# A graph attention layer: the first two weight tiles side by side, another order of ScalarE's and GpSimd's work in a pair step, evacuation by halves

## What is computed

```python
# x: 384 x 1024, 16 heads of 64, 6144 edges
q = x @ wq.T + bq ; k = x @ wk.T + bk ; v = x @ wv.T + bv
q2 = (q @ wiq.T + biq).reshape(N, H, D).transpose(1, 0, 2)
k2 = (k @ wik.T + bik).reshape(N, H, D).transpose(1, 0, 2)
v2 = (v @ wiv.T + biv).reshape(N, H, D).transpose(1, 0, 2)
mask = full((N, N), -inf); mask[src, dst] = softplus(edge_weights)[edge_type - 1]   # the diagonal is always set
scores = einsum('hnd,hmd->hnm', q2, k2) / 8 + mask
out = einsum('hnm,hmd->hnd', softmax(scores), v2).transpose(1, 0, 2).reshape(N, 1024)
return layernorm(x + out @ wo.T + bo)
```

## Time and profile before

| | us |
|---|---|
| median of 3 (306.43 to 307.05) | 306.74 |
| the profiled execution | 306.56 |
| its span, first to last instruction | 304.8 |
| TensorE busy / DVE / ACT / GpSimd | 291.7 / 204.4 / 175.1 / 147.8 |
| granted TensorE clock, share of full | 0.999 |

### The profile page before, as it was taken

The page is one execution under the profiler, slowest core; times in us unless marked ns, Lnnn a source line. Parts: engine busy times, 40 slices in busy tenths (PEclk is TensorE's granted clock), DMA queues, the critical chain, the costliest instruction groups (busy, mean ns, idle before and its releaser), DMA issues. The chain is left out here.

```text
span 304.8 us, 5251 instructions
## 1 busy us (share of the span) xinstructions
PE 291.7 (96%) x1640; PEld 272.4 (89%) x1640; DVE 204.4 (67%) x493; ACT 175.1 (57%) x329; POOL 147.8 (49%) x126
## 2 busy tenths in 40 slices
PE   6899999999999999999999999999999997899992
PEld 6789999999999998888989999999999996678882
DVE  4789856676666674305277888888797888763084
ACT  4843443334443342221488898989898989644432
POOL 4100655655546546478653545454544545944600
PEclk9999999999999999999999999999999999999999
DMA  6886745354652438745021222221222221420013
GB/s 191 311 328 246 264 142 190 97 195 139 207 207 85 148 113 329 292 149 197 10 71 61 78 70 70 69 69 69 69 69 69 69 69 71 139 69 0 2 69 138
DMA packets 14030, 39.83 MB, mean 131 GB/s; under 512 B 3168, under 2 KB 4800, under 8 KB 13888
## 3 DMA queue, kind: packets, MB, share of 16 engines
q1 hardware_dynamic: 11984, 38.91, 36.9%
q0 software_dynamic: 1680, 0.62, 1.0%
q10 hardware_dynamic: 352, 0.13, 0.2%
HBM read 37.44 MB, written 2.21 MB: 130 GB/s over the span
## 5 line engine op out<-in xcount | busy, mean ns | idle before, releaser
L328 POOL DMA_INDIRECT mask_cells<-cell_value,cell x48 | 57.0, 1187 | 60.4 <-DMA mask_cells<-cell_value,cell 31.8
L296 POOL TENSOR_TENSOR w_lo<-w_raw,w_hi 128x1024 fp32r<-128x1024 f32 (+2 forms) x22 | 51.1, 2326 | 63.8 <-DVE probs L748 32.4
L853 PE MATMUL bank<-x_hi,w_hi 128*128 128x384 f32 x192 | 64.5, 336 | 2.9 <-POOL w_lo L296 1.6
L384 ACT ACTIVATE w_hi<-w_raw 128x1024 fp32r<-128x1024 f32 x51 | 52.9, 1054 | 20.4 <-PE bank L862 19.4
L855 PE MATMUL bank<-x_hi,w_lo 128*128 128x384 f32 x192 | 64.2, 334 | 0.0
L854 PE MATMUL bank<-x_lo,w_hi 128*128 128x384 f32 x192 | 64.2, 334 | 0.0
L419 ACT ACTIVATE h_hi<-bank,bcol 128x384 f32 (+1 forms) x24 | 14.0, 582 | 59.7 <-PE bank L855 59.7
L587 DVE TENSOR_TENSOR w_lo<-w_raw,w_hi 128x1024 fp32r<-128x1024 f32 (+2 forms) x32 | 38.3, 1201 | 13.6 <-ACT w_hi L384 11.3
L853 PE MATMUL bank<-h_hi,w_hi 128*128 128x384 f32 x128 | 46.4, 362 | 0.0
L855 PE MATMUL bank<-h_hi,w_lo 128*128 128x384 f32 x128 | 43.0, 336 | 0.0
L854 PE MATMUL bank<-h_lo,w_hi 128*128 128x384 f32 x128 | 42.9, 335 | 0.0
(11 more groups left out here) (103 smaller groups left out, 528.3 us busy)
## 6 DMA issues: line engine op xcount, KB each, us to landing
w_raw<-weights SPq DMA_DIRECT2D x56, 512.0 KB
probs<-key_rows SPq DMA_DIRECT2D x6, 512.0 KB
v<-x_t SPq DMA_DIRECT2D x8, 192.0 KB, 5.7
res<-x_rows SPq DMA_DIRECT2D x1, 1536.0 KB, 6.8
out<-res SPq DMA_DIRECT2D x6, 256.0 KB, 2.0
mask_cells<-cell_value,cell POOLq DMA_INDIRECT x48
mask_cells<-mask SPq DMA_DIRECT2D x1, 576.0 KB, 6.0
mask<-mask_cells POOLq DMA_DIRECT2D x1, 576.0 KB, 4.4
```

The source lines that it names most:

```text
L296: nc.gpsimd.tensor_tensor(lo, w_raw[:, s, cols], hi.bitcast(F32), ALU.subtract)\
L328: nc.gpsimd.indirect_dma_start(out=mask_cells, out_offset=bass.IndirectOffsetOnAxis(ap=cell[:, c:c + 1], axis=0), in_=cell_value[:, c:c + ...
L384: nc.scalar.activation(w_part(t, s, slice(0, F))[0], w_raw[:, s, :], ACT.Copy).then_inc(w_hi_done, 1)
L853: pe.matmul(out_ps, w_hi[:, s, cols], moving_hi, start=(k == 0), stop=False)
```

## The change

- Start: tiles 0 and 1 get accumulators of their own (`first_acc`, banks 4 and 5), and TensorE does both for each block of x. They are loaded and split in halves of 512 columns. ACT issues block 0, the first half of tile 1 and block 3; SP the rest, and the edge arrays, the edge weights and the bias columns behind x. Tile 2 is ahead of the edge columns, tile 3 behind the bias columns, and tiles 4 and 5 ahead of the edge keys. DVE does all low parts; all eight counts of the first group come behind the value table and tile 5's low part.
- Pair step: ACT takes five exponentials, splits the odd weight tile (before, this was the step's last work), and takes the sixth. ACT counts each half of q and k that it evacuates (`half_hi`), and DVE waits for one half at a time. GpSimd subtracts the odd weight tile ahead of `att_low`.
- Around the last pair: ACT splits both weight tiles ahead of the exponentials, GpSimd subtracts both ahead of `v_low` and then waits for all six normalised tiles; DVE masks all six score tiles ahead of the normalisations; TensorE projects with tile `WO_TILE + 1` (left half) and does the last value product of pair 6 ahead of the scores, and the first transposes come behind three projections more.

```diff
         acc = bank[6:8]
+        first_acc = bank[4:6]
...
+            def half_tile(t, h):
+                sp.dma_start(w_raw[:, t, HALVES[h]], weights[t, :, HALVES[h]])\
+                  .then_inc((first_half_loaded, raw_loaded)[h][t], 16)
+            def x_block(k):
                 sp.dma_start(x_raw(k), x_t[:, k, :]).then_inc(x_loaded[k], 16)
-            first_tile(1)
+            half_tile(0, 0)
+            x_block(1)
+            x_block(2)
+            half_tile(0, 1)
+            half_tile(1, 1)
+            for k in range(4, KT):
+                x_block(k)
+            sp.dma_start(er[:, :, :], edge_rows).then_inc(edges_loaded, 16)
+            first_tile(2)
+            sp.dma_start(ec[:, :, :], edge_cols).then_inc(edges_loaded, 16)
+            sp.dma_start(ew[:, :], edge_weights.to_broadcast([P, ETYPES])).then_inc(small_loaded, 16)
             sp.dma_start(bcol[:, :], bias_cols).then_inc(small_loaded, 16)
+            first_tile(3)
+            for s in range(FIRST_TILES):
+                load_tile(RING + s, s)
             sp.wait_ge(edge_prep, 1)
             sp.dma_start(key_rows.rearrange("g (c e) -> (g c) e", e=P), er_key[:, :]).then_inc(scratch_stored, 16)
-            first_tile(2)
             sp.wait_ge(scratch_stored, 16)
             load_rows(0, 0)
-            first_tile(3)
-            for s in range(RING):
+            for s in range(FIRST_TILES, RING):
                 load_tile(RING + s, s)
+            sp.wait_ge(rows_loaded, 16)
             load_rows(1, 1)
...
+                low_part(t + LEAD + 1, s0 + 1)
                 if not (isinstance(j, int) and j < 2):
                     att_low(j - 2)
-                low_part(t + LEAD + 1, s0 + 1)
...
             low_part(WO_TILE + 2, 2)
+            low_part(WO_TILE + 3, 3)
             v_low(PAIRS - 1, 1)
-            low_part(WO_TILE + 3, 3)
+            pool.wait_ge(probs_ready, 2 * NT * PAIRS)
...
-            act.dma_start(er[:, :, :], edge_rows).then_inc(edges_loaded, 16)
-            act.dma_start(ec[:, :, :], edge_cols).then_inc(edges_loaded, 16)
-            act.dma_start(ew[:, :], edge_weights.to_broadcast([P, ETYPES])).then_inc(small_loaded, 16)
+            act.dma_start(x_raw(0), x_t[:, 0, :]).then_inc(x_loaded[0], 16)
+            act.dma_start(w_raw[:, 1, HALVES[0]], weights[1, :, HALVES[0]]).then_inc(first_half_loaded[1], 16)
+            act.dma_start(x_raw(3), x_t[:, 3, :]).then_inc(x_loaded[3], 16)
...
+            def first_high(t, h):
+                act.wait_ge((first_half_loaded, raw_loaded)[h][t], 16)
+                nc.scalar.activation(w_hi[:, t, HALVES[h]], w_raw[:, t, HALVES[h]], ACT.Copy)\
+                    .then_inc((first_half_hi, w_hi_done)[h], 1)
+            def x_high(k):
                 act.wait_ge(x_loaded[k], 16)
                 nc.scalar.activation(x_hi[:, k, :], x_raw(k), ACT.Copy).then_inc(x_hi_done, 1)
-            act.wait_ge(raw_loaded[1], 16)
-            for half, done in zip(HALVES, (first_half_hi, w_hi_done)):
-                nc.scalar.activation(w_hi[:, 1, half], w_raw[:, 1, half], ACT.Copy).then_inc(done, 1)
+            first_high(0, 0)
+            x_high(0)
+            first_high(1, 0)
+            for k in range(1, 4):
+                x_high(k)
+            first_high(0, 1)
+            first_high(1, 1)
+            for k in range(4, KT):
+                x_high(k)
+            high_part(2, 2, 1)
...
-                    ins = nc.scalar.activation((q_high, k_parts)[which][here, 2 * slot + h, :],
-                                               acc[which][here, 0:N], ACT.Identity, bias=bcol[here, ds(u, 1)])
-                ins.then_inc(acc_hi, 1)
+                    nc.scalar.activation((q_high, k_parts)[which][here, 2 * slot + h, :], acc[which][here, 0:N],
+                                         ACT.Identity, bias=bcol[here, ds(u, 1)]).then_inc(half_hi, 1)
...
-                    if isinstance(j, int) and j < 2:
-                        exps(a)
-                    else:
+                    if not (isinstance(j, int) and j < 2):
                         att_half_out(a - 1, 1)
-                        exps(a)
-                if attend:
+                    exps(a, range(0, 5))
+                    split(t + LEAD + 1, s0 + 1, raws)
+                    exps(a, range(5, 6))
...
                 evacuate(t + 1, L1_TILES + 1 + 2 * j, par, 1)
                 if attend:
                     att_half_out(a, 0)
-                split(t + LEAD + 1, s0 + 1, raws)
+                else:
+                    split(t + LEAD + 1, s0 + 1, raws)
...
             split(WO_TILE + 2, 2, (WO_TILE + 2) // RING + 1)
+            split(WO_TILE + 3, 3, (WO_TILE + 3) // RING + 1)
             v_high(a, 1)
             att_half_out(a - 1, 1)
-            exps(a, range(0, 3))
-            split(WO_TILE + 3, 3, (WO_TILE + 3) // RING + 1)
-            exps(a, range(3, 6))
+            exps(a)
...
+            first_low(0, 0)
+            x_low(0)
+            first_low(1, 0)
+            for k in range(1, 4):
+                x_low(k)
+            first_low(0, 1)
+            first_low(1, 1)
+            for k in range(4, KT):
+                x_low(k)
...
+            for t in range(FIRST_TILES):
+                low_part(t + LEAD, t + LEAD)
+                evacuate(t, first_acc[t])
+            low_part(FIRST_TILES + LEAD, 0)
+            evacuate(FIRST_TILES, acc[0])
+            value_table()
+            low_part(FIRST_TILES + 1 + LEAD, 1)
+            evacuate(FIRST_TILES + 1, acc[1])
+            dve.wait_ge(rows_loaded, 16)
+            count_later(0, ds(0, 1), range(GC))
+            choose_cells(0)
...
-                dve.wait_ge(acc_hi, u + 1)
                 for h in range(2):
+                    dve.wait_ge(half_hi, 2 * (u - L1_TILES) + (h + 1))
...
+                last = u is None
+                for i in range(6 if last else 5):
                     mask_scores(a, i)
                 normalise(a, (0, 2))
                 normalise(a, (4,))
-                mask_scores(a, 5)
+                if not last:
+                    mask_scores(a, 5)
...
+            for k in range(KT):
+                pe.wait_ge(x_lo_done, k + 1)
+                for t in range(FIRST_TILES):
+                    if k == 0:
+                        pe.wait_ge(first_half_lo, t + 1)
+                    if k == KT // 2:
+                        tile_ready(t)
+                    ins = by_outputs(first_acc[t][:, 0:N], t, k, x_hi[:, k, :], x_lo[:, k, :])
+                    if k == KT - 1:
+                        ins.then_inc(tile_done, 1)
...
             project(0, 0, left)
             for g in range(KT - VALUES_FROM, 2 * NT - 1):
                 values(a - 1, 0, g)
+            project(0, 1, left)
+            values(a - 1, 0, 2 * NT - 1)
             pe.wait_ge(acc_free, L1_TILES + 2 + 2 * PAIRS)
             scores(a, 1, 0)
             project(0, 0, right)
-            values(a - 1, 0, 2 * NT - 1)
             scores(a, 1, 1)
-            project(0, 1)
+            project(0, 1, right)
             scores(a, 1, 2)
             project(0, 2)
             pe.wait_ge(masked, 2 * NT * PAIRS - 1)
             project(1, 0, left)
             project(1, 1, left)
-            transposes(a, 0)
             pe.wait_ge(masked, 2 * NT * PAIRS)
             project(1, 0, right)
             project(1, 1, right)
             project(1, 2)
+            transposes(a, 0)
+            project(0, 3)
             transposes(a, 1)
-            project(0, 3)
             for g in range(4):
                 values(a, 1, g)
                 transposes(a, g + 2)
```

More of the change, by code:

```diff
@@ L49 @@
 LEAD = 2
-FIRST_COLS = 448
-SHARED_TILES = 2
+FIRST_TILES = 2
 WARM_UP = 16
@@ L182, in gnn_layer @@
         q_doubled = sem("q_doubled")
+        first_half_loaded = [sem(f"first_half_loaded{t}") for t in range(FIRST_TILES)]
         first_half_hi, first_half_lo = sem("first_half_hi"), sem("first_half_lo")
         tile_done = sem("tile_done")
-        acc_hi = sem("acc_hi")
+        acc_hi, half_hi = sem("acc_hi"), sem("half_hi")
         acc_free = sem("acc_free")
@@ L293, in low_part @@
                 pool.wait_ge(w_hi_done, t + 1)
-                cols = pool_cols(t) if isinstance(t, int) and t < SHARED_TILES else slice(0, F)
+                cols = slice(0, F)
                 hi, lo = w_part(t, s, cols)
@@ L411, in group @@
                     t = RING * g + s
-                    late = first and s < LEAD
-                    if not late:
+                    if not (first and s == 0):
                         high_part(t + LEAD, (s + LEAD) % RING, g + 1 + (s + LEAD) // RING)
                     act.wait_ge(tile_done, t + 1)
-                    nc.scalar.activation(h_hi[:, ds(t, 1), :].rearrange("p a n -> p (a n)"), acc[s % 2][:, 0:N],
+                    ps = first_acc[s] if first and s < FIRST_TILES else acc[s % 2]
+                    nc.scalar.activation(h_hi[:, ds(t, 1), :].rearrange("p a n -> p (a n)"), ps[:, 0:N],
```

(48 more changed lines are left out.)

49 lines of the change are left out of this document (19 added, 30 removed).

## The result

| | before | after |
|---|---|---|
| median, us (lowest to highest) | 306.89 (306.43 to 307.82, 4 runs) | 299.64 (299.56 to 299.71, 4 runs) |
| ratio, 95% interval | | 0.976 (0.9736 to 0.9783) |
| profiled execution, its span | 306.56, 304.8 | 299.66, 297.9 |
| mean granted clock of TensorE | 0.999 | 0.997 |

The forecast was 299.9. To see where the 7 us are, I cut the timeline of TensorE at four starts that both traces have (L numbers move, the operations don't): tile 6, the transposes of the first pair, those of the last step of the loop, and the last matmul.

What follows compares the result with a forecast made beforehand. TensorE, busy 96% of the span, was taken as the bound, with gains only where it stands still: start 2.4, loop 1.4, last pair 3.0, sum 6.8, from 306.74 to 299.9 us; range 298.6 to 302.6.

Steps and rivals of the forecast that it cites:

- the loop's 1.4: Pair steps: half evacuations let DVE finish k earlier, removing TensorE's 0.24 wait at the scores in six steps, 1.4 us.
- The start: Up to tile 6: DVE's gapless list after ACT's softplus constants sets tile 6 at 32.75 against 35.18, gain 2.4 us.
- The feared queues: Start, SP's queue: small constants landing at 16 would leave 0.3 gain; edge keys' store and read-back expected without stall.
- (a): Start: constants or rows of keys land late and DVE's backlog leaves a gain of 0.3 to 1; 301.7 us, chance 0.13.
- (d): Start: it is not held by DVE's list; 299.1 us, chance 0.07.
- The first pair: First pair: 0.5 won at the scores is given back at the transposes, where ACT's table load and exponentials set time; 0.
- (b): Pair loop: the 0.24 at L927 is a restart cost, not a wait; 1.4 less gain, 301.3 us, chance 0.10.
- the moved split: Pair step: ACT's 1.05 split fits into its idle 1.16 before the sixth exponential; priced at 0.
- (e): Pair steps: the split delays the sixth exponential by 1.05 each step, costing 7.35; 308.7 us, chance 0.04.
- The odd weight tile on GpSimd: Pair step: subtraction moved ahead of att_low gives the weight tile 4 us more cover, att_low 1.8 later; priced at 0.
- The last pair: Last pair: waits at scores (1.88) and transposes (1.75) go, less 0.3 left at the scores and 0.3 later; gain 3.0 us.
- (c): Last pair: GpSimd's gate delays weight tiles and the last projections by 1.5; 301.4 us, chance 0.06.

Runs made afterwards that it cites:

- e10: Kernel before plus the new start and the half evacuations; split, GpSimd's odd weight tile and last pair at their old places: 304.80 us, ratio 0.9924.
- e8: Kernel after, with DVE's evacuation ahead of the first count in every tile of the loop over groups: 299.32 us, ratio 0.9749.
- e1: Kernel before plus the new start alone; pair steps and last pair as before: 304.95 us, ratio 0.9928.
- e7: Kernel after, with a one-column exponential on ACT before the first pair step, so Exp's table loads early: 298.81 us, ratio 0.9735.
- e3: Kernel after, but DVE waits for both halves of q and k before it evacuates the first: 301.61 us, ratio 0.9818.
- e6: Kernel after, with ACT's split of the odd weight tile one exponential earlier, before the fifth: 305.15 us, ratio 0.9937.
- e4: Kernel after, with ACT's odd-tile split back at the step's end and GpSimd's subtraction behind att_low; halves and last pair stay new: 307.33 us, ratio 1.0011.
- e5: Kernel after, with GpSimd's old order in the last pair and no wait for the six normalised tiles: 300.88 us, ratio 0.9798.
- e2: Kernel before plus the new start and whole pair step; last pair in the old order on all four engines: 302.61 us, ratio 0.9852.
- e9: Kernel after with early Exp table, DVE's evacuation before the first count, and ACT's third transposed tile earlier in the last pair: 297.92 us, ratio 0.9699.

## Why the prediction was right, and where not

**The sum is closer than its terms.** 6.8 was forecast and 6.91 measured, but 0.4 too much at the start and 0.5 too little in the last pair cancel, and the loop's 1.4 was right for a reason that was half wrong. That much is luck.

**The start: the list was right, its beginning wrong, 0.4 too much.** DVE's list holds tile 6, through the evacuation of tile 4, as named. I let this list begin at ACT's softplus constants and run without a gap. Term by term:

| term | forecast | measured |
|---|---|---|
| ACT's softplus constants | 13.9 | 13.36 |
| to the low part of tile 3 | 3.50 | 3.48 |
| to the loop's first low part | 12.88 | 13.80 |
| to tile 6 | 2.47 | 2.57 |

The term mis-sized is the third, and with it the path. DVE idles 0.84 at 20.57 for ACT's evacuation of tile 2, a tile that TensorE began only at 15.60. In the kernel before, DVE came to that evacuation at 26.00, behind the table of values, long after tile 2 was done; the change puts it ahead of the table, and there DVE is the one who waits. I had moved the two counts in the list but not this. So what comes before 20.57 on ACT and DVE has slack, and the 0.54 won at the first term is worth nothing. The table of runs shows it: in the nine kernels that have the new start and DVE's order of the kernel after, tile 6 starts 17.61 to 17.62 behind tile 2, while tile 2 itself moves between 15.60 and 16.10. In e10 ACT starts the constants 0.88 later than in the kernel after (14.24), and tile 6 is still 17.62 behind tile 2. In e8, with one count less in the way, it is 16.95. The feared queues cost nothing: DVE starts its counts without waiting for the rows of keys. Rivals (a) and (d) fall, and e8 moves tile 6 by its order on DVE alone.

**The first pair: right.** The 0.5 won at the scores is given back at the transposes (1.16 there against 0.56 in e1, while the stretch from tile 6 is 124.94 in e1 and 124.97 after). That ACT's table load sets the time there is what e7 shows. The Trainium skill (ScalarE: Activation LUTs, section "What ACT_TABLE_LOAD costs") gives 1283 ns for the load and 1380 more for a drain. The trace agrees with the first (1.28) and shows nothing of the second: from ACT's weight split (150.63 in the kernel after, 150.78 in e7) to its first exponential it is 3.74 with the load and 2.40 without, 1.34 in all.

**The loop: right sum, wrong share.** 1.58 against 1.4, and rival (b) falls with e3. But I gave the whole 1.4 to the halves and priced the moved split at 0, and that step failed. I had noted that the five exponentials would start some 0.4 earlier, and did not ask what would happen if they didn't: by e10 the halves alone are worth 0.1, for the ring of ACT and DVE still takes its 14.8. The forecast came out because both edits were in the change. The cover for the split was as read: its idle 1.16 became 0.22, and e6 shows rival (e) at work as soon as the split stands one exponential earlier.

**The odd weight tile on GpSimd: wrong at 0.** I wrote of 4 us more cover and gave it no price. By e4, without it and the moved split 5.8 are lost in the last pair. No run puts GpSimd's part back alone. An estimate from rows of the kernel after: there its subtraction ends at 252.67, and TensorE takes the tile up at 252.73. Behind `att_low`, which could not start before 251.12 and takes 1.0, a subtraction of 2.4 would end at about 254.5, 1.8 too late. So it is a condition too.

**The last pair: 3.5 against 3.0.** The wait at the scores went entirely, where I had left 0.3 of it. The wait at the transposes went, and 0.27 were left at the third transposed tile (0.3 forecast). Rival (c) falls: GpSimd's first gated low part ends at 267.61, and TensorE begins the projection with it at 267.72. By the rows of e5 the order and gate on GpSimd are worth 1.07 of the rest (47.81 against 46.74).

**Not settled.** e2 against e1 gains 0.93 in the rest with the last pair's order unchanged, where the half evacuation explains 0.5 (the wait there is 1.46 in place of 1.96). In e10, which has the halves but not the early weight tile, the bracket at 259.22 shows 0.45 idle for that tile, and the rest is no shorter (50.26); so the other 0.4 is likely the tile, but no run parts the two there. Of the new order around the last pair only GpSimd's part was undone alone. How the remaining gain divides between ACT's, DVE's and TensorE's order is not shown.

## What to carry to other kernels

Two waits of equal length in one loop step hide each other: removing one paid next to nothing here and both together paid in full. So after removing a wait follow the step once around, to the next operation that another engine releases, before an edit is priced at nothing. Look above all for a ring among the helpers, in which each waits for the other and the busiest engine has no part. The exact place of filler work is worth reading from the trace: the same split was free before the sixth exponential and cost 0.65 a step before the fifth. An order that pulls work forward has conditions on other engines, and taking these away can cost more than the whole change brought, as in e4. And a chain that sets a time in one execution should be held against other executions: a distance that stays the same in nine of them (tile 2 to tile 6) shows the path better than the sum of one.

## What the runs showed of the hardware that I had not expected

**TensorE's clock.** In e4 the granted clock was 1.00 up to the wait of 4.6 between starts at 254.32 and 258.91. In the 3.1 us behind it it was 0.56, most of that at the lower of the two levels (1.2 GHz), and matmuls of 384 columns started every 0.32 us in place of 0.17. Behind the waits of 1.5 to 2.0 in the last pair of e1, e2 and e10 the granted clock was 1.00 in the next 3 us. So a part of the 5.8 lost in e4 is clock: 4.42 is the wait itself, and the twelve matmuls behind it take 4.10 (258.91 to 263.01), where the same twelve take 2.66 in the kernel after (252.73 to 255.39).

**The first real matmul.** In the profiled executions of the eleven kernels with the new start (the kernel after and ten others) it began between 6.27 (e9) and 7.58 (e10). That is not a scatter of the loads: in each of them it starts 0.03 behind the start of the last matmul of the warm-up. What varies is how long the warm-up takes, for the same 32 rows, in e9 and in e10:

```profile
1.13 5.38 PE L906 MATMUL bank<-zeros 128*128 128x128 f32 x32 [1.13 <-DVE zeros L591]
```
```profile
1.13 6.70 PE L903 MATMUL bank<-zeros 128*128 128x128 f32 x32 [1.13 <-DVE zeros L587]
```

The kernel after has 6.02. The starts stand 0.21 apart at first and 0.11 apart later, and the step from one to the other comes at 4.5 in e9, 5.8 in the kernel after and 7.2 in e10. That this is TensorE's clock is inferred from the factor of two, for the windows view gives a granted clock of 1.00 before and after the step. In the nine kernels that have DVE's order of the kernel after, the first matmul moves by 0.80 (6.78 to 7.58), tile 2 by 0.50 and tile 6 by 0.51 (33.21 to 33.72). So the spans of two single traces, as of e8 and e9, can't be compared to 0.1 us.
